# Down product of the experts' low-weight tail over 112 rows instead of 48, and slot notes read by a max over an axis of one

## What is computed

```python
scores = softmax(x @ gate_w.T);  topk_w, topk_ids = top_k(scores, 6)      # 64 experts
gu  = einsum('th,efh->tef', x, w_gate_up)                                  # FFN = 176
act = silu(gu[..., :FFN]) * gu[..., FFN:] * comb[:, :, None]
routed = einsum('tef,ehf->th', act, w_down)
out = layernorm(x + routed + shared)
```

## Time and profile before

| | us |
|---|---|
| median of 3 runs | 1550.52 (1549.78 to 1550.93) |
| the profiled execution, its span | 1551.0 |
| PE busy in the span | 1296.3 (84%) |
| DVE busy | 1096.4 (71%) |
| ACT busy | 841.7 (54%) |
| POOL busy | 685.7 (44%) |
| stretch of the blocks of the experts | from about 1152 to about 1476 |

### The profile page before, as it was taken

The page is one execution under the profiler, slowest core; times in us unless marked ns, Lnnn a source line. Parts: engine busy times, 40 slices in busy tenths (PEclk is TensorE's granted clock), DMA queues, the critical chain, the costliest instruction groups (busy, mean ns, idle before and its releaser), DMA issues. The chain is left out here.

```text
span 1551.0 us, 29748 instructions
## 1 busy us (share of the span) xinstructions
PE 1296.3 (84%) x8828; PEld 1136.6 (73%) x8828; DVE 1096.4 (71%) x2210; ACT 841.7 (54%) x1859; POOL 685.7 (44%) x584
## 2 busy tenths in 40 slices
PE   5899899899899899999899897549809999999800
PEld 3788788788788788788788786536408888888700
DVE  3686776686776676786776777552109999999778
ACT  2565565465565465565565554711107888888701
POOL 3443433443433343543433420057745777777600
PEclk9999999999999999999999999569959999999955
DMA  6320040120140120040300000032237887888574
GB/s 218 94 70 2 29 142 15 41 70 2 32 139 14 42 70 1 21 148 4 112 1 1 1 1 31 1 72 103 104 109 233 242 239 238 239 239 236 173 248 131
DMA packets 100315, 151.51 MB, mean 98 GB/s; under 512 B 10410, under 2 KB 73038, under 8 KB 100196
## 3 DMA queue, kind: packets, MB, share of 16 engines
q1 hardware_dynamic: 89156, 124.75, 26.9%
q0 software_dynamic: 11040, 25.30, 4.8%
HBM read 92.51 MB, written 62.46 MB: 100 GB/s over the span
## 5 line engine op out<-in xcount | busy, mean ns | idle before, releaser
L461 DVE TENSOR_REDUCE neg_max<-scores 128x1 f32<-128x256 f32 (+7 forms) x256 | 192.6, 753 | 196.5 <-PE scores L571 196.5
L379 ACT ACTIVATE pt_hi<-pt 128x512 fp32r<-128x512 f32 (+3 forms) x384 | 174.5, 489 | 245.2 <-PE pt L580 243.6
L429 DVE TENSOR_TENSOR pt_lo<-pt,pt_hi 128x512 fp32r<-128x512 f32 (+3 forms) x384 | 201.3, 552 | 28.5 <-ACT pt_hi L379 12.1
L500 PE MATMUL o_ps<-pt_hi,v_hi 128*128 128x256 f32 (+1 forms) x640 | 196.6, 307 | 21.1 <-DVE o_lo L437 18.5
L356 ACT ACTIVATE probs<-scores,neg_max 128x256 f32<-128x256 f32 (+7 forms) x256 | 189.8, 742 | 43.3 <-DVE neg_max L461 29.9
L318 POOL TENSOR_TENSOR turned<-taken,cos 128x512 f32<-128x512 f32 x80 | 108.1, 1352 | 177.0 <-ACT taken L366 176.8
L580 PE MATMUL pt<-ident,probs 128*128 128x128 f32 x1152 | 171.0, 276 | 16.5 <-DVE pt_lo L429 14.9
L501 PE MATMUL o_ps<-pt_lo,v_hi 128*128 128x256 f32 (+1 forms) x640 | 181.4, 284 | 0.0
L502 PE MATMUL o_ps<-pt_hi,v_lo 128*128 128x256 f32 (+1 forms) x640 | 181.0, 283 | 0.0
L1061 POOL DMA_INDIRECT results_dram<-y_sb,dest x134 | 149.3, 1114 | 35.5 <-issue 30.0
L310 POOL TENSOR_TENSOR q_lo<-turned,q_hi 128x512 fp32r<-128x512 f32 x64 | 83.2, 1299 | 183.9 <-ACT q_hi L389 183.9
(11 more groups left out here) (186 smaller groups left out, 3698.3 us busy)
## 6 DMA issues: line engine op xcount, KB each, us to landing
rows_dram<-empty SPq DMA_DIRECT2D x32, 919.1 KB
up_raw<-in_up SPq DMA_DIRECT2D x69, 368.0 KB, 3.8
x_in<-rows_dram SPq DMA_DIRECT2D x68, 258.0 KB, 3.3
parts<-results_dram SPq DMA_DIRECT2D x16, 768.0 KB, 9.5
down_raw<-in_down SPq DMA_DIRECT2D x69, 128.0 KB, 2.7
down_raw<-in_down_tail SPq DMA_DIRECT2D x69, 112.0 KB, 3.5
w_raw<-in_w SPq DMA_DIRECT2D x8, 768.0 KB, 8.6
x_raw<-in_xT SPq DMA_DIRECT2D x8, 512.0 KB, 4.5
```

The lines of the kernel that those rows point to most:

```text
L379: nc.scalar.activation(pt_hi[m // 2 % 2][:, a:z, P * (m % 2):P * (m % 2) + P], pt_ps[c % 2][:, 0:P * (z - a)].rearrange("p (k q) -> p k q" ...
L429: nc.vector.tensor_tensor(pt_lo[m // 2 % 2][part], pt_ps[c % 2][:, 0:P * (z - a)].rearrange("p (k q) -> p k q", q=P), pt_hi[m // 2 % 2][pa ...
L461: nc.vector.tensor_reduce(neg_max[:, n % 4:n % 4 + 1], scores_ps[n % 2][:, 0:key_tiles(n) * P], AX.X, ALU.max, negate=True).then_inc(max_m ...
L500: nc.tensor.matmul(out, lh, rh, start=first, stop=False)
```

## The change

Four edits, all in `experts`:

1. The matmul of L1327 takes rows 0 to 111 of `hidden_hi` and of `down_lo` instead of rows 0 to 47. Rows 64 to 111 add the product lo*lo of the tail; rows 48 to 63 are zero in `hidden_hi`.
2. `note` and its tile and semaphore are gone. `address(n)` makes `dest` and `weight` directly from `x_in`, each by a tensor_reduce with max over an axis of length one (three instructions become two).
3. `address` has another place: in DVE's loop it was address(k), last; now it is address(k-1), behind x_lower(k+1), where note(k+1) stood. `load_rows(n)` waits for `addressed` of block n-3 instead of `noted`.
4. In POOL's loop `landed(m-1)` stands ahead of `send(m)` instead of behind it.

```diff
@@ block.sync
             def load_rows(i, u):
                 n, buf, _ = block_of(i, u)
                 sp.wait_ge(x_turned, done(n, 3))
-                sp.wait_ge(noted, done(n, 3))
+                sp.wait_ge(addressed, done(n, 3))
@@ block.gpsimd
             with pool.Fori(1, triples) as i:
                 for u in range(-2, 1):
                     split_up(i, u + 4)
+                    landed(i, u - 1)
                     send(i, u)
-                    landed(i, u - 1)
             split_up(triples, 2)
             for u in range(-2, 1):
+                landed(triples, u - 1)
                 send(triples, u)
-                landed(triples, u - 1)
@@ block.vector
-            def note(i, u):
+            def address(i, u):
                 n, buf, count = block_of(i, u)
                 dve.wait_ge(rows_in[buf], 16 * count)
-                dve.tensor_copy(goes_with[buf][:], x_in[buf][:, :, H:ROW]).then_inc(noted, 1)
-
-            def address(i, u):
-                n, buf, _ = block_of(i, u)
-                dve.wait_ge(noted, done(n))
                 dve.wait_ge(y_sent, done(n, 3))
-                dve.tensor_copy(dest[buf][:], goes_with[buf][:, :, 0])
-                dve.tensor_copy(weight[buf][:], goes_with[buf][:, :, 1]).then_inc(addressed, 1)
+                dve.tensor_reduce(dest[buf][:], x_in[buf][:, :, H:H + 1], AX.X, ALU.max)
+                dve.tensor_reduce(weight[buf][:], x_in[buf][:, :, H + 1:ROW], AX.X, ALU.max).then_inc(addressed, 1)
@@
                 for u in range(1, 4):
                     hidden_lower(i, u - 1)
                     x_lower(i, u + 1)
-                    note(i, u + 1)
+                    address(i, u - 1)
                     split_up(i, u + 2)
                     hide(i, u)
                     split_down(i, u + 1)
-                    address(i, u)
             hidden_lower(triples, 0)
+            address(triples, 0)
@@ block.tensor, down(i, u)
-                    mm = nc.tensor.matmul(y, hidden_hi[buf][0:TAIL, 1, tok], down_lo[buf][0:TAIL, 1, :], start=False, stop=True)
+                    mm = nc.tensor.matmul(y, hidden_hi[buf][0:LOW_AT + TAIL, 1, tok], down_lo[buf][0:LOW_AT + TAIL, 1, :],
+                                          start=False, stop=True)
```

More of the change, by code:

```diff
@@ L957, in experts @@
         y_sb, dest, weight = three("y_sb", [P, SUB, H]), three("dest", [P, SUB], I32), three("weight", [P, SUB])
-        goes_with = three("goes_with", [P, SUB, 2])
         RING, GROUP_TILES = 8, 4
@@ L971, in experts @@
         up_in, down_in, rows_in, y_out = ([sem(f"{name}{i}") for i in range(3)] for name in ("up_in", "down_in", "rows_in", "y_out"))
-        x_turned, x_hi_made, x_split, noted = sem("x_turned"), sem("xt_hi_made"), sem("xt_split"), sem("noted")
+        x_turned, x_hi_made, x_split = sem("x_turned"), sem("xt_hi_made"), sem("xt_split")
         up_hi_made, up_split = sem("up_hi_made"), [sem(f"up_split{k}") for k in range(HK)]
@@ L1173, in _ @@
             dve.sem_inc(x_split, 3)
-            dve.sem_inc(noted, 3)
             dve.sem_inc(addressed, 3)
@@ L1230, in _ @@
             x_lower(0, 0)
-            note(0, 0)
             x_lower(0, 1)
-            note(0, 1)
             split_up(0, 1)
@@ L1239, in _ @@
             hide(0, 0)
-            address(0, 0)
             with dve.Fori(0, triples) as i:
```

## The result

The changed kernel takes **1602.29 us** (median of 4 runs, 1602.03 to 1607.43) against 1550.63 for the kernel before beside it: a ratio of 1.034, with an interval of 1.0323 to 1.0356. It is slower by 52 us. The forecast was 1617, with 1582 to 1650 as its range.

The account below looks back on a forecast made before the run. PE bounds the kernel before at 4.50 us a block; two loops, through load_rows and POOL's sends, raise it to 5.5: 2.0 + 64 x 1.00 = 66 us on 1551.0 gives 1617, range 1582 to 1650.

Parts of the forecast that it names:

- What bounds before: In the experts' blocks PE sets the pace, busy 249.60 of 250 us, at 4.50 us a block.
- Edit 1: Matmul of L1327: 48 rows lose PE 0.56 us a block, 38 us at most; now only adds to PE's idle time.
- Edit 2: Notes on DVE: some 0.6 us less a block, up to 0.5 perhaps lost at L1204; counts nothing in the sum.
- Edit 3: Deciding term: load_rows waiting for address behind x_lower closes a loop of 5.46 us a block, 5.2 to 5.7.
- the landing: Time for load_rows to land, inside that loop: taken as 3.1 us, between 2.8, 3.0 and 3.3.
- Loads of weights: Up and down weights queued on SP behind load_rows move with it and still land before ACT needs them.
- Edit 4: POOL's sends wait for landings, a second loop: 1.48 + 3.9 + 0.16 = 5.54 us, 4.9 to 5.8.
- The sum: Period 5.5 us: first held turn 2.0 us late, 64 more 1.00 each, 66 us on 1551.0, giving 1617.
- Rival A: Quick landings, rows after 2.7 us and sends after 3.4: loops 5.06 and 5.04, 1591 us; chance 0.15.
- B: Rival: held loads do not bind, only the gains count, 4.1 us a block, 1525 us; chance 0.04.
- C: Rival: PE's clock stays at 0.50 (1.2 GHz), 6.7 us a block, 1694 us; chance 0.09.
- Turns under 5 us apart: Sign of a wrong prediction in the profile after: landings would be shorter than any row seen.

Follow-up runs that it names:

- e1: Kernel before with only the down matmul of L1327 widened to 112 rows: 1601.16 us against 1619.32, ratio 0.9893.
- e3: Kernel before with only the notes read from x_in by two reduces, behind x_lower, load_rows waiting for them: 1673.57 us, ratio 1.0357.
- e4: Changed kernel with send ahead of landed again: 1662.27 us, ratio 1.0275 to the kernel before.
- e6: Kernel before with the note taken by one tensor_reduce instead of the copy, in its old place: 1551.24 us, ratio 1.0005.
- e5: Kernel before with the wider matmul and the note taken by one tensor_reduce in its old place: 1532.61 us, ratio 0.9882.
- e11: Changed kernel with one more unused 256-column reduce on DVE ahead of the two reading the notes: 1685.72 us, ratio 1.0412 to the kernel before.
- e9: Changed kernel with send ahead of landed and address(k-1) ahead of x_lower(k+1): 1654.98 us, ratio 1.0225 to the kernel before.
- e2: Kernel before with only landed put ahead of send in POOL's loop: 1704.60 us, ratio 1.0536.
- e7: Changed kernel with address(k) back at the end of DVE's pass, landed still ahead of send: 1677.50 us, ratio 1.082 to the kernel before.
- e10: Kernel before with wider matmul, note by one reduce, and POOL's send ahead of split_up: 1645.52 us, ratio 1.0165.

## Why the prediction came out

**What bounds before.** Right. PE at 249.60 of 250 was the bound, and e1 moved it.

**Edit 1.** Right in the size of the stall (0.21 and 0.31 to 0.12 and 0.12), which e1 turns into 18 of the 38 us that it allowed at most, and in that it can't pay for the rest. Wrong in that it "only adds" to PE's idle time: e3 beside e4 gives it 11 us in the changed kernel, by way of the turn to x_lower, 1.53 against 1.32 as medians. In the prediction's own sum this made no error, because the 1.36 it took for that distance assumed all others to be early, which holds only with edit 1; that this came right is luck.

**Edit 2.** Right: nothing in the sum, and nothing in the time (e6). The caution that L1204 may take over the wait was borne out, 0.53 to 1.05 us (e5).

**Edit 3.** Right as the term that decides: edits 2 and 3 alone give the ratio (e3), and so do edits 1 to 3 (e4); edit 2 by itself gives nothing (e6), and lengthening the loop lengthens the block (e11). Term by term, against the turn shown above: turn to x_lower 1.36 predicted and 1.32 seen; x_lower and the reduces 0.84 and 0.82; SP 0.16 and 0.23; landing 3.1 and 2.87 from issue to turn (2.77 as the median of the middle blocks), 2.6 as the median landing alone. **The mis-sized term is the landing**: 0.3 us too long with the hop to the turn, 0.5 without it. It was taken between the quietest and the busiest rows of before, and both stood above what the steady changed kernel shows. With 2.6 in its place the prediction's loop is 4.96, a little short of the 5.16 of the middle blocks, since SP takes 0.07 more and the hop from the landing to the turn, some 0.15, had no term. With the medians of the trace, 1.32 + 0.82 + 0.23 + 2.77, it is 5.14. The Trainium skill (DMA: Bandwidth & Descriptors, Anatomy of one DMA) has 2.0 us plus the bytes at 436 GB/s for a transfer that the general engine issues, an estimate of 2.6 for these 258 KB; this one is issued by SP. The median of 2.6 agrees; the 3.3 of before, for the same bytes, doesn't.

**Loads of weights.** Wrong: the prediction let them "still land before ACT needs them". ACT waits 33.2 us in 48 blocks for up_raw, 0.69 each. It costs little in the changed kernel, where ACT has that time free and the chain passes over this transfer in three of the 53 middle blocks; in e9, with the first loop shorter, ACT waits 40.5 us in 40 blocks between 1250 and 1450, and it is what seems to stand next.

**Edit 4.** The mechanism is right: POOL waits for the landing in every block, in e2 and in the changed kernel. Its terms were off in both directions. The second send lands after 2.3 us in the changed kernel and not 3.9; from first to second send it is 1.77 and not 1.48; and from the landing to the next send it is 0.95 and not 0.16, which was read from rows where nothing was waited for. Together that is 5.04 and not 5.54, just under the 5.16 of the rows. That both loops were predicted nearly equal and came out nearly equal is thus partly luck. The prediction also called landings of sends under 2.9 us "below any row", against its own 2.2 from the earlier trace rows. Had it kept one loop instead of two, the sum would be the same, because it took the longer.

**The sum.** 2.0 + 64 x 1.00 = 66 was computed for the span; 2.5 + 64 x 0.72 = 48.3 was found up to the last turn, and 49.2 for the span. The forecast has 18 us too much in the 64 turns and 1.4 too little in the rest, which makes the 17 us between 1617 and the span of 1600.2. The forecast's own range, 1596 to 1646 from loops of 5.2 to 6.0, leaves out its 2 us for the first turn; with them it is 1598 to 1649. Rival A had the landings right for the rows (2.7) and missed by 11 us on the other side, 1591: its loop of 5.06 is 0.1 short of the middle blocks, and it gave no price to the start and the end, where the blocks take 5.58 us, about half of the miss each.

**The rivals.** B is out: the load is held in every block. C is out for this kernel: PEclk was 1.00 (2.4 GHz) from 1200 to 1450 with PE at 77%, and only at the start (0.72 in 1168 to 1180) and behind 1500 was it lower; the start was so before too. In e2 and e7 the grant between 1250 and 1450 was 0.94 and 0.91, between the two levels of 1.2 and 2.4 GHz, with PE busy for 85% and 72%, but there POOL's loop accounts for the whole period. "Turns under 5 us apart" or "above 6" would have been the signs of a wrong prediction; 5.16 lies between.

## What to carry to other kernels

Before the last reader of a buffer is moved, write down the loop that its release closes (release, issue, landing, first use, last use) and compare its length with the period; as long as the loads run a whole block ahead the landing is free, and with one pass less it is paid in every block, however idle the engines are. A small instruction inside such a loop costs most of its time even on an engine with a quarter of its time free (e11), and a wait for landings put ahead of the next issue makes a loop of its own, whose length depends on the landings (5.0 us here, 5.9 in e2, 6.5 in e7). Don't take such a wait for absent because the engine shows no idle time: the sequencer can wait while the engine still works on the instruction before. A matmul over few contraction rows among full ones can be the dearer one: over 112 rows in place of 48 this kernel takes 1.1% less.

## What the runs showed of the hardware

- The load of rows landed after 2.6 us in the changed kernel at a DMA share of 0.70 and in e7 at 0.56, after 3.3 before at 0.81 and after 3.1 in e5 at 0.85; the recorded one of the first two took 3.0 before and 2.8 in the changed kernel, with little beside it. The share alone doesn't order these.
- The second send of a block lands after 2.3 us in the changed kernel, 2.6 us behind the issue of the up weights; after 3.9 before, 1.6 us behind it; after 3.5 in e2, close beside it; after 4.2 in e7, 0.4 us behind it. The last sends of the changed kernel, with no loads beside them, took 2.1 to 2.4. No run varied this alone.
- From the landing of a send for which POOL waited to the start of its next send it took 0.94 to 0.95 us (e2, e7, and the end of the changed kernel, 1516.20 to 1517.15).
- A DVE operation that reads two operands from SBUF is held up by POOL's indirect DMA issue as well as by POOL's arithmetic, and by both in a row: 1.92 us for 0.53 of work (e10), and L1218 or its like 1.75 in e2 and 1.85 in e7 for 0.68. In the changed kernel the first send's issue takes 1.2 to 1.8 us, beside DVE's L1211, and the second's 0.98; POOL's half of the split, started 0.05 us behind DVE's, takes 1.32 instead of 0.97. Reduces of 2 or 4 columns took 0.15 us beside any of these.
